# Output-projection blocks inside the score stream of an attention and FP4 layer kernel

## The reference, cut to what matters

```python
x = _layernorm(x + attn(x, ...))       # x: (2, 2048, 256) float32
x = _layernorm(x + ffn(x, weight, bias, delta_w, delta_act))

# attn
Q, K = linear(cat([q_in, conv1d(q_in)])), linear(cat([k_in, conv1d(k_in)]))   # 16 heads of 16
V = linear(x, Wv_w, Wv_b)
tau, delta = sigmoid(pointwise(gelu(depthwise(x)))) twice
scores = einsum("bhqd,bhkd->bhqk", Q, K) / sqrt(DK) * tau[..., None] + delta[:, :, None, :]
out = linear(softmax(scores) @ V, out_w, out_b)

# ffn
x_q = mxfp4_pseudo_quant(x, delta_act)     # blocks of 32, rounded to FP4 steps
w_q = mxfp4_pseudo_quant(weight, delta_w)
return einsum("bsd,od->bso", x_q, w_q) + bias
```

## Time and profile before

| | us |
|---|---|
| median of three runs | 1696.35 |
| profiled execution, whole time | 1700.33 |
| profiled execution, span first to last instruction | 1698.5 |
| PE busy | 1642.5 (97%) |
| DVE busy | 1538.2 (91%) |
| ACT busy | 1322.7 (78%) |
| POOL busy | 74.6 (4%) |
| mean granted PE clock, share of full | 0.981 |

### The profile page before, as it was taken

How to read it: one execution, slowest core, us unless ns; L and a number is a source line. 1 busy time by engine, 2 the same in 40 slices (tenths; PEclk the granted TensorE clock), 3 DMA queues, 4 the chain that set the end, 5 groups by cost and what they waited for, 6 DMA issues and landing times.

```text
span 1698.5 us, 33654 instructions
## 1 busy us (share of the span) xinstructions
PE 1642.5 (97%) x13972; PEld 745.1 (44%) x13978; DVE 1538.2 (91%) x1638; ACT 1322.7 (78%) x2389; POOL 74.6 (4%) x133
## 2 busy tenths in 40 slices
PE   8999989999999999999999999999999999998977
PEld 7677754333333333333333333333333333334466
DVE  5588977999999999999999999999999999985797
ACT  3688723888888888888888888888888888885534
POOL 3000003000000000000000000000000000001110
PEclk9899997999999999999999999999999999999998
DMA  3376436000600060006002400322050000002232
GB/s 111 91 191 171 123 91 95 9 8 8 76 16 8 8 84 8 8 9 83 8 14 30 66 8 8 51 44 61 29 71 21 8 8 8 8 8 86 82 101 75
DMA packets 46961, 84.73 MB, mean 50 GB/s; under 512 B 9116, under 2 KB 21020, under 8 KB 44092
## 3 DMA queue, kind: packets, MB, share of 16 engines
q1 hardware_dynamic: 44952, 82.49, 22.6%
q10 hardware_dynamic: 1856, 0.09, 0.1%
HBM read 51.36 MB, written 30.67 MB: 48 GB/s over the span
## 4 chain that ended last, share of the span: by engine, by line
PE 62%; DVE 21%; ACT 1%; issue 1%; ACTq 0%; POOL 0%; DVEq 0%
PE ps L846 26%; PE ps L833 20%; DVE mx L218 17%; PE ps L208 11%; PE ps L869 1%; PE ps L914 1%; PE ps L867 1%; PE ps L820 0%; DVE stats L1059 0%; DVE work L1094 0%; DVE work L1093 0%; ACT e L989 0%; DVE work L1085 0%; DVE small L1080 0%; DVE scr L1089 0%
## 5 line engine op out<-in xcount | busy, mean ns | idle before, releaser
L218 DVE TENSOR_REDUCE mx<-ps 128x2 f32<-128x1024 f32 x1024 | 1230.4, 1223 | 60.6 <-PE ps L208 51.2
L989 ACT ACTIVATE e<-ps 128x512 f32<-128x512 f32 x2048 | 1110.3, 596 | 210.5 <-PE ps L833 170.4
L846 PE MATMUL ps<-e,v_grp 128*32 128x256 f32 x8192 | 657.7, 393 | 0.2 <-issue 0.2
L833 PE MATMUL ps<-q,k 52*128 52x512 f32 x2048 | 525.3, 499 | 4.0 <-ACT e L989 4.0
L208 PE MATMUL ps<-k,q 50*128 50x512 f32 x2048 | 420.8, 404 | 11.1 <-DVE mx L218 6.5
L833 PEld LDWEIGHTS ps<-q,k 52*128 52x128 f32 x2048 | 199.4, 184 | 430.8 <-ACT e L989 400.0
L846 PEld LDWEIGHTS ps<-e,v_grp 128*32 128x32 f32 x8192 | 162.1, 108 | 359.2 <-issue 202.4
L208 PEld LDWEIGHTS ps<-k,q 50*128 50x128 f32 x2048 | 198.9, 188 | 39.7 <-DVE mx L218 31.0
L608 PE MATMUL ps<-x_p,m_p 128*128 128x512 f32 x576 | 143.1, 405 | 0.0
L608 PEld LDWEIGHTS ps<-x_p,m_p 128*128 128x128 f32 x576 | 109.1, 193 | 31.0 <-issue 6.5
L440 DVE SCALAR_TENSOR_TENSOR hid<-x_c,dw_w,hid 128x512 f32<-128x512 f32 x128 | 88.5, 746 | 13.2 <-ACT hid L382 13.2
(11 more groups left out here) (127 smaller groups left out, 621.8 us busy)
## 6 DMA issues: line engine op xcount, KB each, us to landing
k<-k_parts SPq DMA_DIRECT2D x42, 256.0 KB
q<-q_parts SPq DMA_DIRECT2D x42, 256.0 KB
k_parts<-k_sp SPq DMA_DIRECT2D x16, 512.0 KB, 5.1
q_parts<-q_sp SPq DMA_DIRECT2D x16, 512.0 KB, 4.6
att<-ev SPq DMA_DIRECT2D x32, 256.0 KB
x_c<-in_x_t SPq DMA_DIRECT2D x8, 514.0 KB, 6.4
tau_r<-tau_rows SPq DMA_DIRECT2D x16, 256.0 KB
x_in<-in_x SPq DMA_DIRECT2D x8, 512.0 KB, 3.7
```

The lines of the kernel that those rows point to most:

```text
L218: nc.vector.tensor_reduce(mx[:, j % 2, :, jh, qt, kc], ps[:, b0:b0 + 2, :], AX.X, ALU.max).then_inc(s_free, 1)
L833: nc.tensor.matmul(ps[:, st_bank(n), :], k_set[r, g % 2, jh, kt * P:(kt + 1) * P], q_set[r, g % 2, jh, lo:lo + CH], start=True, stop=True) ...
L846: last = nc.tensor.matmul(ps[32 * h:32 * (h + 1), 0, PVW * part:PVW * (part + 1)], v_grp[:, kt, h, :], e[:, x % E_BUFS, h * CH + PVW * par ...
L989: nc.scalar.activation(e[:, x % E_BUFS, h * CH:(h + 1) * CH], ps[:, st_bank(n), :], ACT.Exp).then_inc(e_ready, 1)
```

## The change

- **Stage one, DVE:** `v_bias(0, 0)` moves from the head of the chunk loop to behind `side_bias_of(0, 1)`.
- **Blocks of chunks 0 and 1 become items** ("o"): those of chunk 0 stand in item iteration 27 behind units 5, 13, 21 and 29, those of chunk 1 in iteration 28. PE writes each into the bank of its item, DVE copies it to `y_of[n]` (128x256); moments and the first norm of these chunks read `y_of[n]`, not PSUM. Items of an iteration are spread over its 32 slots by their number (up to 37); in iteration 30 the last `rows` item goes to the slot behind the 24.
- **Blocks of chunks 2, 3 and 4** stand at x = 494 to 497, 498 to 501 and 507 to 510. The square roots stand behind x = 495 (chunks 0 and 1 together), 501 and 505.
- **SP and POOL:** chunks 2 and 3 are loaded in iteration 29, set 1 of the sums (chunks 4 and 5) in iteration 30; POOL's products for chunks 0 and 1 stand in iteration 24, for 2 and 3 in iteration 30. There are four sets of sums.
- **A fifth norm buffer** (`y_of` has five), and behind stage two the order is `transposed(n)`, `linear(n)`, `project(n + 5)`, for chunks 5 to 7.

```diff
+        O_AT = {(27 + n, 8 * a + 5): ("o", n, a) for n in range(2) for a in range(TT)}
@@ stage one, vector
                 for n in range(NCHUNK):
                     more = n + 1 < NCHUNK
-                    if n == 0:
-                        v_bias(n, 0)
                     if more:
                         tap(n + 1, 0, range(4))
...
                         side_bias_of(0, 1)
+                        v_bias(n, 0)
...
-        Z_SETS = ((0, NQ), (NQ, NCHUNK - 1), (NCHUNK - 1, NCHUNK))
+        Z_SETS = ((0, NQ), (NQ, NQ + 2), (NQ + 2, NQ + 3), (NQ + 3, NCHUNK))
...
-            PROJECT_AT = [LAST - 3, LAST - 3, LAST - 2, LAST - 2] + [LAST - 1 + m for m in range(3 * TT)]
-            ROOT_AT = {LAST + 1: 0, LAST + 5: 1, LAST + 10: 2}
+            PROJECT_AT = {x0 + a: (n, a) for n, x0 in ((2, LAST - 2), (3, LAST + 2), (4, LAST + 11)) for a in range(TT)}
+            ROOT_AT = {LAST - 1: (0, 1), LAST + 5: (2,), LAST + 9: (3,)}
@@ tensor
+                        if isinstance(u, tuple):
+                            n, a = u[1:]
+                            pe.wait_ge(s_free, s - 1)
+                            if a == 0:
+                                loaded(n)
...
+                            block_of(ps[:, s_bank(s), 0:D], n % 2, a).then_inc(s_full, 1)
+                            return
...
-                        due = min(PER, len(items) - issued)
-                        slots = SLOTS if due == PER else SLOTS * 3 // 4
+                        goal = items.index((i + 2, LEAD)) if i + 2 < NIT else len(items) - 1
+                        due = goal - issued
+                        slots = SLOTS * 3 // 4 if i == NIT - 2 else SLOTS
...
                     for n in range(NCHUNK):
                         transposed(n)
-                        if n + EARLY < NCHUNK:
+                        linear(n)
+                        if n + EARLY + 1 < NCHUNK:
                             for a in range(TT):
-                                project(n + EARLY, a)
-                        linear(n)
+                                project(n + EARLY + 1, a)
@@ vector
+                            if isinstance(u, tuple):
+                                n, a = u[1:]
+                                dve.wait_ge(s_full, s + 1)
+                                nc.vector.tensor_copy(y_of[n][:, a], ps[:, s_bank(s), 0:D]).then_inc(s_free, 1)
+                                continue
...
-                    moments(0, 0, o_full, o_bank(0))
+                    z_reciprocal(dve, 1)
+                    moments(0, 0)
+                    moments(0, 1)
                     scale_shift(0, 0)
                     normalised(0)
@@ gpsimd
+                        if i in (Z_AT + 8, Z_AT + 14):
+                            normalise(2 * (i == Z_AT + 14))
+                            normalise(2 * (i == Z_AT + 14) + 1)
@@ sync
+                        if i == NIT - 2:
+                            sp.wait_ge(att_stored, 32 * i)
+                            z_load(sp, 1)
...
+                        if i == NIT - 3:
+                            next_load(2)
+                            next_load(3)
```

More of the change, by code:

```diff
@@ L685, in layer_kernel @@
         CD = TT * D
-        z_loaded = [sem(f"z_loaded{k}") for k in range(3)]
-        z_stored = [sem(f"z_stored{k}") for k in range(3)]
+        z_loaded = [sem(f"z_loaded{k}") for k in range(4)]
+        z_stored = [sem(f"z_stored{k}") for k in range(4)]
         z_ready = sem("z_ready")
@@ L730, in layer_kernel @@
             tiles = lambda flat: flat.rearrange("p (a d) -> p a d", a=TT)
-            y_of = [y[:, 0], y[:, 1]] + [tiles(v_second[:, CD * p:CD * (p + 1)]) for p in range(2)]
+            y_of = [y[:, 0], y[:, 1]] + [tiles(v_second[:, CD * p:CD * (p + 1)]) for p in (0, 1, 3)]
             xq_of = [xq[:, 0], xq[:, 1]] + [tiles(v_second[:, 2 * CD + CD // 2 * p:2 * CD + CD // 2 * (p + 1)].bitcast(BF16)) for p in range(2)]
@@ L802, in _, with block_of, loaded @@
                 def _(pe):
+                    def block_of(dst, p, a):
+                        nc.tensor.matmul(dst, ones3[:], bias3[:, 0, 0, :], start=True, stop=False)
+                        nc.tensor.matmul(dst, ident_f[:], x_in[:, p, a, :], start=False, stop=False)
+                        for c in range(CT):
+                            last = nc.tensor.matmul(dst, a_t[p][:, c, P * a:P * (a + 1)], wo_t[:, c, :], start=False, stop=(c == CT - 1))
+                        return last
+                    def loaded(n):
+                        pe.wait_ge(x_in_loaded[n % 2], 16 * (n // 2 + 1))
+                        pe.wait_ge(a_norm, n + 1)
                     def s_item(s):
                         j, u = items[s]
+                        if isinstance(u, tuple):
[3 more added lines that the diff above has]
+                                loaded(n)
+                            if (n, a) == (0, 0):
+                                pe.wait_ge(bias_ready, 1)
+                            block_of(ps[:, s_bank(s), 0:D], n % 2, a).then_inc(s_full, 1)
+                            return
                         if u == "ft":
@@ L852, in project @@
                     def project(n, a):
-                        p = n % 2
                         if a == 0:
[L856 to L859, removed]
+                            loaded(n)
+                            if n < EARLY:
                                 pe.wait_ge(s_free, len(items))
[L861 to L866, removed]
-                        nc.tensor.matmul(dst, ident_f[:], x_in[:, p, a, :], start=False, stop=False)
-                        for c in range(CT):
-                            last = nc.tensor.matmul(dst, a_t[p][:, c, P * a:P * (a + 1)], wo_t[:, c, :], start=False, stop=(c == CT - 1))
+                            else:
+                                pe.wait_ge(y_ready, 3 if n == EARLY else n)
+                        last = block_of(tok(o_bank(n), a), n % 2, a)
                         if a % 2:
@@ L1084, in scales @@
                         link(nc.vector.reciprocal(rs, sc))
[L1085 removed]
+                        link(nc.vector.tensor_tensor(blocks(work[:]), blocks(y_of[n % 5]), wide(rs), ALU.mult))
                     def steps(n):
@@ L1195, in _ @@
                                 refill(g + 1, c)
-                    for n in range(NCHUNK):
+                    for n in range(EARLY, NCHUNK):
                         normalise(n)
```

85 lines of the change are left out of this document (50 added, 35 removed).

## The result

The changed kernel takes 1710.97 us (median, 1709.02 to 1720.69), the kernel before 1696.16 on the same chip: a ratio of 1.0087, 95% interval 1.0055 to 1.012. It is slower by 14.8 us, where 8.9 us faster was forecast. The profiled execution took 1711.01, with a span of 1709.2; before it was 1698.5. Of the 14.8 us the two profiles show 10.7, since before's profiled execution was 4 us above its median. Medians and ratios in this document are of undisturbed executions; one of `e5_act3` (1888.63 us) and one of `e8_btail` (3454.27 us) are left out.

The account below looks back on a forecast made before the run. PE's issue order was taken to bound stage two, DVE behind it. Last transposition +10.7 us, from there to scales(4) 20.1 gained, 0.5 added behind: -8.9 from 1696.35 gives 1687.4 us, range 1681.5 to 1694.5.

Parts of the forecast that it names:

- What bounds it: PE's issue order bounds stage two with DVE 3% behind; PE still paces the end, DVE behind stage two.
- Stage one: DVE's taps of chunk 1 fill its 12.51 us hole, so pointwise(1) runs unslowed: gain 2.6 us, bounds 0 and 6.2.
- Blocks in the stream: Eight blocks on PE in stage two at 1.42 plus 0.12 waiting each: 12.3 us, bounds 11.4 and 14.1.
- the last interval: End of the stream: the last rows item stands one slot later, one bare slot more, 1.0 us.
- R: The last transposition, before at 1528.44, forecast 10.7 us later; in R to s, s is the start of scales(4).
- R to chunk 4's last block: On PE from the last transposition to x = 510: steps, blocks, table waits 65.0, plus 1.7 clock; 66.7 us.
- the clock: PE at half clock behind the new table waits: about 2 us lost, twice up to 3.7; 1.7 taken.
- DVE's wait at `moments(0, 4)`: DVE waits some 9 us there for PE's blocks of chunk 4, named the new bound.
- Behind it: From scales(4) to the end: same chain for chunks 5 to 7, new order costs 0 to 0.5 a chunk; 0.5 added.
- a tail that is no longer 75.6: Sign of being wrong: the time from scales(4) to the end differs from 75.6 us.
- The stream breaks: Rival, chance 0.07: item waits paid in full behind every block, from 2.66 a block; at 3.4, 15 us more, 1702.
- A dip and a late root: Rival, chance 0.12: both new PE waits lower the clock (3.7) and DVE is late for the third root; 1692.

Follow-up runs that it names:

- e5_act3: The changed kernel with finish(n - 1) ahead of turn(n) on ACT for n from 1 to 3 only, PE's order as changed; 1699.99 us, ratio 1.0007.
- e8_btail: The kernel before with only the tail's order changed to transposed(n), linear(n), project(n + 4); 1711.6 us, ratio 1.0069.
- e4_paired: e1_order with stream blocks not counted in the spreading, each issued in the slot of the unit that follows it; 1698.42 us, ratio 0.9998.
- e6_c4: e1_order with chunk 4's blocks four steps earlier, at x = 503 to 506; 1696.67 us, ratio 0.9979.
- e1_order: The changed kernel with PE's old order back behind stage two: transposed(n), project(n + 4) for n from 1 to 3, linear(n); 1698.79 us, ratio 1.0003.
- e3_vbias: The kernel before with the stage-one part alone, v_bias(0, 0) behind side_bias_of(0, 1); 1700.46 us, ratio 1.0016.
- e7_all: e6_c4 with the pairing of e4_paired added; 1694.19 us, ratio 0.9963.
- e9_c2: e7_all with chunk 2's blocks one step earlier, at x = 493 to 496; 1690.09 us, ratio 0.9961.
- e10_best: e9_c2 with the tail of e5_act3 (PE's and ACT's order) in place of that of e1_order; 1690.59 us, ratio 0.9947.
- e2_act: The changed kernel with finish(n - 1) ahead of turn(n) on ACT for all n, PE's order as changed; 1708.39 us, ratio 1.007.

## Why the prediction was wrong, point by point

- **What bounds it:** right. PE paces the stream, PE's pace decides up to the blocks of chunk 4, DVE behind stage two.
- **Stage one:** right, -3.0 in the stretch for -2.6.
- **Blocks in the stream:** the mechanism right, the term too small. I took 1.54 a block; 1.84 was paid (14.7 / 8), beyond the upper bound of 1.76. The bare block takes 1.51 there, not the 1.42 of the earlier trace rows. On top come the 0.34 of waiting that a double slot costs, which I had read rightly from the earlier trace rows and then cut to 0.12 on the ground that a block as slot-mate frees DVE; every displaced unit made a double slot with another unit and paid it in full. `e4_paired` recovers 0.16 of it. For the last interval I had 1.0, "one bare slot more"; it grew by 2.5, which is two slots at 1.24, one of them taken from an earlier interval (0.8). From the split at 1119.05 (before) and 1113.37 (after) to R it is +16.4, forecast +13.3.
- **R:** +10.7 forecast, +10.7 found, by luck. The stream cost 3.1 more, and the changed execution came 5.7 us earlier to that split; 2.2 us of that stand already ahead of the first `v_bias`, where nothing differs, and 3.0 are stage one.
- **R to chunk 4's last block:** loads hidden, waits of 2.37, 1.03 and 2.49 (forecast 2.8, 1.0, 2.8): right. The failed term is the clock: "a block and a step at half clock lose about 2 us, twice up to 3.7; I take 1.7". The lower clock lasted 3.7 us behind the first wait, but 10.7 behind the third, with PE busy all the time, and the last moments came at R + 70.9 instead of R + 66.7. By PE's own starts it cost 5.2 us for the 1.7: 3.5 of the 4.2. `e6_c4`, which shortens the third wait to 1.0 us and has R to s 3.7 us shorter, speaks for it too, though it moves blocks as well.
- **DVE's wait at `moments(0, 4)`:** named as the new bound, some 9 us forecast, 12.4 found. Right, and `e6_c4` shows that it bound, and that a wait of 7.3 us for the root is the next bound.
- **Behind it: the step that failed.** "The second norm's moments need `linear(1)` about 2 us after it ends by my count, so the new order costs 0 to 0.5 a chunk." I followed the moved instructions on PE to their consumer on DVE only. What had to be followed is everything that then stands behind them: `transposed(n + 1)` behind the blocks of chunk n + 5, these behind ACT's norm, ACT's `turn` behind `transposed`, the root behind `turn`, DVE's `steps` behind the root. This path cost 15.8 us more than forecast. `e5_act3` takes one link out and the 16.9 us are gone (91.9 to 75.0), `e1_order` takes another out (91.9 to 77.7). The prediction had named "a tail that is no longer 75.6" as what would show it wrong, but gave it no mechanism and no chance.
- **The rivals:** none held. "The stream breaks" was on the right side for another reason; a block cost 1.84, not 2.66. "A dip and a late root" was right that both waits bring the lower clock, and still priced it too low (5.2 us for its 3.7); the third root was not late.

Without the failed step the change would still not have been faster by 8.9: `e1_order` and `e5_act3`, with the tail mended, measure 1.0003 and 1.0007. The stretches give -2.9, within those intervals: -3.0 in stage one, +16.4 in the stream and -16.3 behind R. The forecast was too good by the blocks and slots of the stream (3 us) and by the clock (3.5).

What stays open: why the clock goes low behind the same wait in one execution and not in another, why the time of `e3_vbias` shows nothing of its 3 us, and which of the two mended tails is the better.

## What to carry to other kernels

When an instruction is moved on one engine, list for every engine what stands behind each instruction that waits for it, and go round until nothing new is late: here a root of 0.30 us, with its input ready, held up DVE 17.8 us through two other queues. A wait that hides a table change or a transfer wants work right ahead of it: with a block before the exponentials' break PE's wait went from 2.4 or 2.5 us to 1.0 or 1.3, and the clock behind it was 1.00 in `e7_all`, `e9_c2` and `e10_best` and 0.86 in `e6_c4`, where it had been 0.50 to 0.61. And work taken from a tail into a stream bound by the same engine is paid in full there, with something on top for the pairing: 1.84 us a block for a bare 1.51.

## What the runs showed of the hardware

**TensorE's clock differs between executions of the same code.** The table by stretches for 272 to 297 us, at the start of stage two where the programs are the same, in the kernel before, in `e1_order` and in `e4_paired`:

```profile
272.00:297.00 25.00, 24.55 (x156) 9.51 (x154) 15.40 (x14) 13.13 (x25) 3.16 (x5) 0.73 0.97 114
```
```profile
272.00:297.00 25.00, 24.55 (x222) 9.45 (x222) 21.28 (x19) 21.65 (x41) 0.00 (x0) 1.00 0.84 99
```
```profile
272.00:297.00 25.00, 24.55 (x132) 8.84 (x132) 13.06 (x11) 12.84 (x25) 1.21 (x2) 0.61 0.87 107
```

PE is busy 24.55 us in each and gets 156, 222 and 132 matmuls done, at a granted clock of 0.73, 1.00 and 0.61. The second split of the maxima falls at 311.9, 302.2 and 312.7 us, in `e7_all` at 315.6: 13 us of spread, beside a scatter of the kernel before from 1690.8 to 1707.8 us over 23 runs. This is why R moved by 10 us between profiles of kernels with the same stream (1533.46 in `e1_order`, 1543.51 in `e5_act3`; 9.1 of it stand at the second split already, 302.2 and 311.3), and why the stretches are compared here, not the marks.

**The clock can stay low for long behind a short wait.** Behind PE's wait of 2.49 us the clock was 0.54, near the lower of the two levels (1.2 GHz), for 10.7 us with PE busy throughout; behind 3.3 us it was 1.00, behind 1.30 us 1.00. It is no accident of one execution: the five profiles with the wait of 2.5 us at that place (the changed kernel, `e1_order`, `e2_act`, `e4_paired`, `e5_act3`) have 0.50 to 0.58 over the 10.7 us from R + 50, those with a wait of 1.03 there 0.86 (`e6_c4`) and 1.00 (`e7_all`, `e9_c2`, `e10_best`). Nor does the length of the wait decide alone: behind the wait of 1.23 us at R the clock fell to 0.50 in `e1_order` and `e10_best` and stayed at 1.00 in the others. The Trainium skill, "TensorE: Matmul & The Clock Gate", section "What's actually happening", has activity release the lower rate; those 10.7 us of a fully busy PE and the 25 us above show a busy PE that stayed at it or came back to it.

**Two table changes with two roots between them** took 3.09 us of ACT (timeline of ACT), exponentials directly behind: 1.28 a load, nothing to be seen of a drain.

```profile
1543.75 1.28 ACT L965 ACT_TABLE_LOAD   x1
1545.04 0.49 ACT L965 ACTIVATE std<-mv,eps_col 128x4 f32<-128x4 f32 x2
1545.55 1.28 ACT L1006 ACT_TABLE_LOAD   x1
1546.84 2.07 ACT L1006 ACTIVATE e<-ps 128x512 f32<-128x512 f32 x4
```
